# Routed tiles of a mixture of experts: the spreads on SyncE six tiles ahead, and an expert's three weight loads one per tile

## The reference

```python
y = clip(einsum('blc,oc->blo', x * styles, weight) * dcoefs + bias, -256, 256)
shared = silu(xf @ sh_gate_w) * (xf @ sh_up_w) @ sh_down_w        # xf: y as (8192, 512)
topk_idx, w = route(xf)                                            # 8 experts of 64
sorted_x = xf[tok]                                                 # rows sorted by expert
h = silu(ragged_dot(sorted_x, gate_w, sizes)) * ragged_dot(sorted_x, up_w, sizes)
o = ragged_dot(h, down_w, sizes) * w
out = x + shared + zeros.at[tok].add(o)
```

## Time and profile before

| | |
|---|---|
| time, median of 3 runs | 3974.17 us (3964.74 to 3979.28) |
| the profiled execution | 3965.72 us, span 3964.0 us |
| PE, PEld busy | 3733.3 us (94%), 3040.4 us (77%) |
| DVE, ACT, POOL busy | 2235.7 us (56%), 1495.3 us (38%), 1946.4 us (49%) |
| granted TensorE clock, mean | 0.977 of full speed |
| DMA | 550.56 MB, mean 139 GB/s |

### The profile page before, as it was taken

One profiled execution on the slowest core, in us unless ns is written; L12 is line 12 of the kernel. 1 busy time (PEld: TensorE's weight loads), 2 busy tenths in 40 slices (PEclk: granted clock), 3 DMA queues, 4 the chain that ended last, 5 costly groups with the idle time before them and its releaser, 6 DMA issues.

```text
span 3964.0 us, 91393 instructions
## 1 busy us (share of the span) xinstructions
PE 3733.3 (94%) x17024; PEld 3040.4 (77%) x17025; DVE 2235.7 (56%) x4612; ACT 1495.3 (38%) x3339; POOL 1946.4 (49%) x1601
## 2 busy tenths in 40 slices
PE   7999999999999959999999999999999999999987
PEld 5877877878787848878878878787878778777775
DVE  4655555555555645555555555555555555566554
ACT  3222222222222214444444444444444444444443
POOL 1453333333333425655556556555656555555554
PEclk9999999999999979999999999999999999999998
DMA  5121112112111228888889888988888898899887
GB/s 181 51 57 44 44 54 54 44 44 65 44 44 54 44 70 181 182 196 177 177 191 184 182 189 182 200 176 188 178 190 185 187 201 175 194 204 204 198 185 158
DMA packets 589051, 550.56 MB, mean 139 GB/s; under 512 B 133625, under 2 KB 443265, under 8 KB 588929
## 3 DMA queue, kind: packets, MB, share of 16 engines
q0 software_dynamic: 136112, 281.38, 36.5%
q10 hardware_dynamic: 291584, 140.58, 13.9%
q1 hardware_dynamic: 161234, 127.04, 11.7%
HBM read 229.07 MB, written 179.19 MB: 103 GB/s over the span
## 4 chain that ended last, share of the span: by engine, by line
PE 46%; DMA 7%; issue 4%; ACTq 3%; DVE 2%; SPq 1%; DVEq 1%; ACT 1%; POOLq 0%; POOL 0%
PE bank L1231 30%; PE bank L1249 14%; DMA x_split<-x_rows 4%; PE bank L1240 2%; ACTq L1341 2%; DMA raw_d<-in_L_ffn_down_w_dram 1%; DMA out_dram<-o_rows,to_row 1%; DVE w_dn_l L30 1%; DMA lists<-slot_list 1%; DMA x_rows<-y_rows,from_row 1%; DVE x_cols L1407 0%; ACTq L1074 0%; SPq L1074 0%; ACT x_h L1289 0%; DVE w_gu_l L30 0%
## 5 line engine op out<-in xcount | busy, mean ns | idle before, releaser
L1193 POOL DMA_INDIRECT out_dram<-o_rows,to_row x532 | 879.5, 1653 | 278.2 <-issue 230.0
L1177 POOL DMA_INDIRECT x_rows<-y_rows,from_row x539 | 543.9, 1009 | 840.6 <-DMA x_split<-x_rows 605.5
L428 POOL DMA_INDIRECT slot_list<-ent,pos x512 | 503.9, 984 | 862.7 <-PE bank L454 385.4
L1231 PE MATMUL bank<-w_gu_h,x_h 128*128 x2128 | 844.3, 397 | 86.1 <-DVE x_l L30 42.7
L1231 PE MATMUL bank<-w_gu_h,x_l 128*128 x2128 | 840.3, 395 | 0.0
L1231 PE MATMUL bank<-w_gu_l,x_h 128*128 x2128 | 839.7, 395 | 0.0
L1407 DVE STREAM_TRANSPOSE x_cols<-x_split 128x512 f32<-128x512 f32 x535 | 580.1, 1084 | 293.9 <-DMA x_split<-x_rows 293.2
L1414 DVE TENSOR_TENSOR e_hf<-bank,e_sg 128x256 f32<-128x256 f32 x532 | 225.2, 423 | 684.4 <-ACT e_sg L1295 366.2
L1231 PEld LDWEIGHTS bank<-w_gu_h,x_h 128*128 128x128 f32 x2128 | 406.4, 191 | 186.4 <-issue 99.1
L1249 PE MATMUL bank<-w_dn_h,e_h_h 128*128 x1064 | 468.1, 440 | 33.7 <-DVE e_h_l L30 20.5
L1231 PEld LDWEIGHTS bank<-w_gu_l,x_h 128*128 128x128 f32 x2128 | 406.9, 191 | 86.7
(11 more groups left out here) (242 smaller groups left out, 5946.7 us busy)
## 6 DMA issues: line engine op xcount, KB each, us to landing
x_split<-x_rows ACTq DMA_DIRECT2D x1072, 128.0 KB
xin<-in_x_dram SPq DMA_DIRECT2D x16, 1024.0 KB
y_rows<-yrow SPq DMA_DIRECT2D x64, 256.0 KB
stage_d<-in_x_dram SPq DMA_DIRECT2D x16, 1024.0 KB
out_dram<-stage_d SPq DMA_DIRECT2D x16, 1024.0 KB
raw_gu<-in_L_ffn_gate_w_dram SPq DMA_DIRECT2D x29, 512.0 KB
raw_gu<-in_L_ffn_up_w_dram SPq DMA_DIRECT2D x29, 512.0 KB
raw_d<-in_L_ffn_down_w_dram SPq DMA_DIRECT2D x29, 512.0 KB
```

Source lines behind the costliest of these rows:

```text
L428: nc.gpsimd.indirect_dma_start(slots, bass.IndirectOffsetOnAxis(ap=pos[v][:, t, k:k + 1], axis=0), ent[v][:, t, k, :], None).then_inc(scat ...
L1177: nc.gpsimd.indirect_dma_start(xg[u // 2][:, u % 2, :], None, y_rows, bass.IndirectOffsetOnAxis(ap=from_row[u][:].bitcast(U32), axis=0)).t ...
L1193: nc.gpsimd.indirect_dma_start(out, bass.IndirectOffsetOnAxis(ap=to_row[u][:].bitcast(U32), axis=0), og[u][:], None, compute_op=ALU.add).t ...
L1231: last = nc.tensor.matmul(b_gu[u % 2][:], xp[a][:, u % 2, k, :], wgu[b][:, bass.ds(place, 1), k, :].rearrange("p a n -> p (a n)"), start=( ...
```

## The change

The spreads go from ACT's queue to SP's. SP's step j now loads the list of tile j+12, issues for even j the spread of tiles j+6 and j+7, then, in an If of its own each, the down matrix if tile j+4 is the first of its expert, the up matrix if tile j+5 is, and the gate matrix if tile j+6 is. The gather runs eight tiles ahead of POOL's step instead of seven, and rows_from nine instead of eight. The waits are the same as before in each part: the spread waits for both gathers and until tile j+3 is turned.

```diff
-            AHEAD = UN
+            LIST_AHEAD, SPREAD_AHEAD, LOAD_AHEAD = 12, 6, 6
...
+                def spread(j, v, g):
+
+                    for u in (2 * v, 2 * v + 1):
+                        sp.wait_ge(x_ld[u], 16 * (g + 1))
+                        sp.nop(nofuse=True)
+                    if not isinstance(j, int) or j >= UN:
+                        sp.wait_ge(dve_turned, j - 2)
+                        sp.nop(nofuse=True)
+                    for a in range(QD):
+                        sp.dma_start(x_split[v][a * SQ:(a + 1) * SQ, :, :, :].rearrange("c i u e -> c (i u) e"),
+                                     xg[v][:, :, a * P:(a + 1) * P]).then_inc(x_moved[v], 16)
+
-                def weights(j, is_first):
+                def weights(j, is_first, part):
 
                     with sp.If(is_first > 0):
                         order = field(sp, j, 1, E)
                         e = field(sp, j, 2, E - 1)
                         half = order & (RAW - 1)
-                        sp.wait_ge(split, 3 * order + 1)
-                        sp.nop(nofuse=True)
+                        if part == 0:
+                            sp.wait_ge(split, 3 * order + 1)
+                            sp.nop(nofuse=True)
                         if not isinstance(j, int) or j > 0:
...
+                            if part == 0:
+                                sp.wait_ge(raw_gu_ld, 32 * order)
+                                sp.nop(nofuse=True)
+                            if part == 2:
+                                sp.wait_ge(raw_d_ld, 16 * order)
+                                sp.nop(nofuse=True)
+                        if part < 2:
+                            sp.dma_start(raw[0][:, bass.ds(half, 1), :, part * H:(part + 1) * H].rearrange("p a k n -> p (a k) n"),
+                                         (gate_w, up_w)[part][bass.ds(e, 1)].rearrange("e (k p) h -> p (e k) h", p=P)
+                                         ).then_inc(raw_gu_ld, 16)
+                        else:
+                            sp.dma_start(raw[1][:, bass.ds(half, 1), :, :].rearrange("p a k n -> p (a k) n"),
+                                         down_w[bass.ds(e, 1)].rearrange("e (k p) h -> p (e k) h", p=P)).then_inc(raw_d_ld, 16)
...
-                def step(g, u, is_first):
-                    n = g * UN + u
-                    load_list(n, u, g)
-                    weights(n - AHEAD, is_first)
+                def step(g, u, turn):
+                    j = g * UN + u
+                    load_list(j + LIST_AHEAD, (u + LIST_AHEAD) % UN, g + (u + LIST_AHEAD) // UN)
+                    if u % 2 == 0:
+                        spread(j + SPREAD_AHEAD, (u + SPREAD_AHEAD) % UN // 2, g + (u + SPREAD_AHEAD) // UN)
+                    for part in (2, 1, 0):
+                        n = j + LOAD_AHEAD - part
+                        if not isinstance(j, int) or n >= LOAD_AHEAD:
+                            weights(n, turn.first(u + LOAD_AHEAD - UN - part), part)
...
-                    gather(g + 1 + (u + 3) // UN, (u + 3) % UN)
+                    gather(g + 2, u)
...
-                    if u % 2 == 0:
-                        spread(j + UN, u // 2, g + 1)
...
-                    rows_from(j + 2 * UN, u, g + 2)
+                    rows_from(j + 2 * UN + 1, (u + 1) % UN, g + 2 + (u + 1) // UN)
```

More of the change, by code:

```diff
@@ L1127, in weights @@
                         half = order & (RAW - 1)
-                        sp.wait_ge(split, 3 * order + 1)
-                        sp.nop(nofuse=True)
+                        if part == 0:
+                            sp.wait_ge(split, 3 * order + 1)
+                            sp.nop(nofuse=True)
                         if not isinstance(j, int) or j > 0:
-                            sp.wait_ge(raw_gu_ld, 32 * order)
-                            sp.nop(nofuse=True)
-                            sp.wait_ge(raw_d_ld, 16 * order)
-                            sp.nop(nofuse=True)
@@ L1136, in weights @@
-                        for n, w in enumerate((gate_w, up_w)):
-                            sp.dma_start(raw[0][:, bass.ds(half, 1), :, n * H:(n + 1) * H].rearrange("p a k n -> p (a k) n"),
-                                         w[bass.ds(e, 1)].rearrange("e (k p) h -> p (e k) h", p=P)).then_inc(raw_gu_ld, 16)
-                        sp.dma_start(raw[1][:, bass.ds(half, 1), :, :].rearrange("p a k n -> p (a k) n"),
-                                     down_w[bass.ds(e, 1)].rearrange("e (k p) h -> p (e k) h", p=P)).then_inc(raw_d_ld, 16)
@@ L1149, in _ @@
                     if n == 1:
-                        weights(0, field(sp, 0, 3, 1))
+                        for part in range(3):
+                            weights(0, field(sp, 0, 3, 1), part)
+                spread(0, 0, 0)
                 for n in range(UN, 2 * UN):
                     load_list(n, n - UN, 1)
-                for n in range(1, UN):
-                    weights(n, field(sp, n, 3, 1))
-                for n in range(2 * UN, LISTS):
-                    load_list(n, n % UN, n // UN)
-                    weights(n - AHEAD, field(sp, n - AHEAD, 3, 1))
+                    if n == UN + 1:
+                        spread(2, 1, 0)
+                for n in range(1, LOAD_AHEAD):
+                    for part in range(3):
+                        weights(n, field(sp, n, 3, 1), part)
+                for n in range(2 * UN, LIST_AHEAD):
+                    load_list(n, n % UN, n // UN)
+                spread(UN, 0, 1)
+                sp.wait_ge(words, 1)
+                for g in range(2):
+                    turn = Turn(sp, g + 1)
+                    for u in range(UN):
+                        step(g, u, turn)
                 last_turn = field(sp, 0, 5, NTURN - 1)
-                sp.wait_ge(words, 1)
-                with sp.Fori(LISTS // UN, NTURN + 2) as g:
-                    with sp.If(last_turn >= g - 2):
-                        turn = Turn(sp, g - 1)
+                with sp.Fori(2, NTURN) as g:
+                    with sp.If(last_turn >= g):
+                        turn = Turn(sp, g + 1)
                         for u in range(UN):
-                            step(g, u, turn.first(u))
+                            step(g, u, turn)
                 for u in range(UN):
-                    sp.wait_ge(list_ld[u], 16 * last_turn + 48)
+                    sp.wait_ge(list_ld[u], 16 * last_turn + 16 * (1 + LIST_AHEAD // UN))
+                    sp.nop(nofuse=True)
+                for v in range(UN // 2):
+                    sp.wait_ge(x_moved[v], 16 * QD * last_turn + 16 * QD * (3 - v))
                     sp.nop(nofuse=True)
@@ L1202, in _ @@
                 pool.wait_ge(tab_ld, 16)
-                for n in range(UN + 3):
+                for n in range(2 * UN):
                     gather(n // UN, n % UN)
@@ L1330, in end_weights @@
                     weights_high(order, order & (RAW - 1), order & (RING - 1), 2)
-                def spread(j, v, g):
-                    for u in (2 * v, 2 * v + 1):
-                        act.wait_ge(x_ld[u], 16 * (g + 1))
-                        act.nop(nofuse=True)
-                    if not isinstance(j, int) or j >= UN:
-                        act.wait_ge(dve_turned, j - 2)
-                        act.nop(nofuse=True)
-                    for a in range(QD):
-                        act.dma_start(x_split[v][a * SQ:(a + 1) * SQ, :, :, :].rearrange("c i u e -> c (i u) e"),
-                                     xg[v][:, :, a * P:(a + 1) * P]).then_inc(x_moved[v], 16)
                 def step(g, u, turn):
@@ L1356, in step @@
                         end_weights(turn.order(u + 2))
-                    if u % 2 == 0:
-                        spread(j + UN, u // 2, g + 1)
-                spread(0, 0, 0)
-                spread(2, 1, 0)
                 act.wait_ge(words, 1)
@@ L1477, in _ @@
                 turn_x(2, 2, 0)
+                rows_from(2 * UN, 0, 2)
                 turn = Turn(dve, 0)
```

3 lines of the change are left out of this document (2 added, 1 removed).

## The result

| | before | after |
|---|---|---|
| time, median | 3976.73 us (3964.74 to 3986.67, 4 runs) | 4458.65 us (4454.87 to 4464.37, 4 runs) |
| ratio | | 1.1215, 95% interval 1.118 to 1.1249 |
| profiled execution, span | 3965.72 us, 3964.0 us | 4459.48 us, 4457.8 us |
| granted clock, mean | 0.977 | 0.947 |

The change makes the kernel 482 us slower, where 195 us were forecast, with 4440 us as the upper end of the range. All of it lies in the stage of the routed tiles, which is 493 us longer. The first fence is the page's busy times, which answer to the earlier trace rows, and its summary of the chain that ended last; the second the gate/up matmuls (count, ns min/median/max, first and last start), to set beside the earlier trace rows.

A forecast was written before the change was run, and what follows sets the result against it. TensorE bounds the routed-tile stage now (2461 us, some 150 of it stalls); SyncE would become the bound, 531 x 4.5 + 266 = 2656 us, +195. So 3965.7 + 195 = 4160 us, range 3905 to 4440.

The forecast's parts named there:

- part 1: Spread leaves ScalarE: frees 1.47 us a tile there, buys nothing in quiet stretches, helps next to a weight load.
- Part 2: Spread six tiles ahead: some 11.7 us less 2.6 of issue nearly cover a 10.3 us landing; list waits are covered.
- Part 3, the price of an issue: Two spread issues a tile on SyncE: 0.86 us at SyncE's own price, 1.35 at ScalarE's, kept for the range.
- Part 3, the step: SyncE's step with spread issues, two more Ifs, waits and nops: 4.4 to 4.65 us a tile, taken as 4.5.
- the stretch of 1.39: SyncE's quiet step of 2.0 us measured 2.77 a tile, so its work was taken to run 1.3 to 1.39 slower.
- The loads: Weight loads on SyncE: 7.8 to 11.2 us for an expert's three parts; 9.5 x 28 = 266 us taken.
- The sum: SyncE needs 531 x 4.5 + 266 = 2656 us for a 2461 us stage: +195 us, 4160 us.
- the SP case: SyncE becomes the bound of the routed-tile stage: 4160 us, own range 4060 to 4525, chance 0.54.
- A: Rival: SyncE keeps up at 3.6 us a tile, the late spread at loads is covered: 3910 us, chance 0.30.
- B: Rival: SyncE at TensorE's pace, or spreads land late behind loads in its queue (over 12 us): 3966 us, chance 0.16.
- C: Rival: the spread can't run six ahead, as it waits for tile j+3; partly true, in the sums, no chance given.
- The signs that I had named: SyncE's waits shrink from 29 us to nearly none, spread issues back to back, 4.4 us a tile, VectorE/GpSimd awaiting late issues.

The follow-up runs named there:

- e13: The changed kernel run again unedited, on a chip where SyncE's instructions paused: 4442.23 us, 1.1198 of the kernel before.
- e14: The changed kernel with lists 32 deep instead of 16, on a chip with pauses: 4179.68 us, 1.0537 of the kernel before.
- e8: The changed kernel with GpSimd's scatter put ahead of its gather, on a chip without pauses: 4044.87 us, 1.0216 of the kernel before.
- e15: The changed kernel with GpSimd's scatter ahead of its gather, on a chip with pauses: 4220.79 us, 1.0633 of the kernel before.
- e17: The changed kernel run a third time unedited, on a chip without pauses: 4331.81 us, 1.0949 of the kernel before.
- e3: The changed kernel with an expert's three loads in one block behind one If, spreads still on SyncE: 4348.24 us, 1.0973 of the kernel before.
- e10: The kernel before with only GpSimd's scatter put ahead of its gather: 3992.62 us, 1.0089 of the kernel before.
- e11: The changed kernel with an expert's loads in one block and GpSimd's scatter ahead of its gather: 3901.05 us, 0.9851 of the kernel before.
- e12: The changed kernel with lists loaded by ScalarE, loads in one block and GpSimd's scatter ahead of its gather: 3868.09 us, 0.9777 of the kernel before.
- e7: The changed kernel with lists loaded by ScalarE and an expert's loads in one block: 3948.36 us, 0.9962 of the kernel before.
- e1: The changed kernel with lists 32 deep instead of 16, in an earlier comparison, with pauses: 4180.22 us, 1.0530 of the kernel before.

## Why the prediction was wrong, step by step

Where the 482 us went, from runs on one chip (e13, e14): 4442.2 - 3967.7 = 475 us, of which 4442.2 - 4179.7 = 262 us are the ring and 212 us SyncE's run time. What the pauses have in the latter is shown for the other break of the ring: e8 and e15, the same kernel, are +83 us without pauses and +253 with them, 170 us for the pauses. The counts bear out most of the 170: SyncE's work is 0.20 us a tile more in e15 (106 us) and its waits 38 us more. Lists 32 deep were never run without pauses; if 83 us were left there too, 129 of the 212 would be pauses, an estimate. Without pauses (e17, e8) the parts are 292 us of ring and 83 of run time.

**What bounds the kernel, and part 1.** Nothing in the runs speaks against them. That the move off ScalarE buys nothing in the quiet stretch was not tried by itself.

**Part 2, the step that failed.** "Lists are read 12 ahead of SP's step instead of 16 ...; both are covered by three tiles of run-ahead as long as SP isn't late." I took SyncE's wait for the scatters, 785 us, as time to spare. It is a place in a queue: whatever is put behind it on SyncE hangs on a scatter. The term that I put at nothing is the wait for a scatter ahead of each spread, and it is 262 us of the 475 (e13, e14). I costed the wait for the list and for the gather each by itself and never followed them round: list behind scatter, spread behind list, gather behind spread, scatter behind gather. The trace before would have given the lap: a scatter's landing (5.2 us by the median, not among my rows), two of SyncE's steps at my own 4.4 to 4.65 us a tile, a spread's landing of 4.59, and 2 us of GpSimd (not among my rows either): about 21 us against the 17.4 of four tiles. It is 21.3. My own clause "as long as SP isn't late" was broken by my own forecast that SyncE would be late in every turn.

**Part 3, the price of an issue.** I took 0.40 us, that of SyncE's other issues; it is 0.637, ScalarE's 0.645. The price that I kept for the range was right and the value taken wrong.

**Part 3, the step.** All the same SyncE's work a tile came out as forecast. A turn of four tiles without loads takes 17.9 us of work in the changed kernel (the median), 4.48 us a tile; I took 4.5. That is luck, for two errors cancel. Issues and gaps cost 1.33 us where I had 0.86. The two Ifs cost 0.59 by e3 (15.6 us a turn), 0.30 each, which is what I had. By the same count SyncE worked 2.68 us a tile in the kernel before, so 2.68 + 1.33 + 0.59 and my 0.10 to 0.15 for waits and nops would be 4.7. But the 2.68 hold pauses: 278 of some 0.67 us in the stage before are 0.36 us a tile. The changed kernel has 129, 0.19 us a tile less, and 4.7 - 0.19 is the 4.5. I had taken the stretch of 1.39 to grow with the work; where there are no pauses, SyncE works 2.15 us a tile with the spreads on ScalarE (e10), the same additions give 4.2, and e17 has 4.22.

**The loads.** 2.0 to 2.3 us of SyncE for each part, some 6.4 us an expert, where I took 9.5: 180 us, not 266.

**The sum.** 531 x 4.48 + 180 = 2560 us of work. e14, with the ring open, has a stage of 2684 us of which SyncE waits 124, the same 2560. The sum had 2656; the times are +212 us and +195. So "SP becomes the bound" was right in kind, and near in size to what is left when the ring is open (by luck in part, since 129 of those 212 us are pauses by the estimate above). What it left out was the 262 us of the ring. The 4459 us lie inside the 4060 to 4525 that I gave the SP case, but not for its reason: its upper end came from dearer issues and loads.

**The rivals.** A (3910 us, SyncE keeps up) was wrong for this change. e11, where SyncE has the time and no ring, gives 59 us, near the 56 that A had worked out from the late spreads at the loads; no run shows that it is these, and e12 gives more. B rested in part on the order of SyncE's queue. In the changed kernel, whose loads are spread out, a spread issued after them (the last at 1838.60 us) wasn't late, by the chain from 1844 to 1852 us:

```profile
1845.72 4.69 DMA x_split<-x_rows
```

The kernels with one block of loads put it to the test. In e7 a spread is issued right behind three loads, with them still under way; the slowest of this run (SyncE's timeline, then the chain):

```profile
2285.11 0.38 SPq L1141 DMA_DIRECT2D raw_d<-in_L_ffn_down_w_dram  x1
2285.92 3.81 SPq L1121 DMA_DIRECT2D x_split<-x_rows  x4
```

```profile
2289.04 11.42 DMA x_split<-x_rows
```

Of such spreads, whose fourth issue comes within 7 us of all three loads, e7 has 22, which land after 7.7 us by the median (5.3 to 11.4), and e12 22 after 8.2 us (up to 10.7). In the kernel before, 15 of them on ScalarE's queue took 9.7 us (4.7 to 11.3). So sharing the queue with the loads cost nothing that shows, and B's landings of over 12 us came in neither. The Trainium skill, "DMA: Bandwidth & Descriptors", section "Queues, rings and completion order", would let the spread stand behind the loads of its queue. All 44 did land after the last load of their block, but so did the 15 on the other queue, so these traces don't tell the rule from its absence. The Trainium skill, same page, section "Issuing engines are not separate DMA queues", calls the sequencer time usually small; here it is 2.7 us for a pair of tiles, and with the Ifs and loads beside it the bound once the ring is open. C (it can't run six ahead) I had priced by the wait for the turned tile; SyncE hardly ever waits there (1.0 us in all up to 4100 us). It was the wait for the scatter that held it back.

**The signs that I had named.** SyncE's waits in 80 us fell from 29.1 to 5.6, the issues of the spread stand one after another, and VectorE and GpSimd wait for a late issue: all as said, and all true of the ring as well. None told the two apart. What did was the sum over the stage: an engine that is the only bound doesn't wait 280 us for scatters that stand behind its own spreads.

## What to carry to other kernels

An engine's idle time at a wait is only free for work that may hang on that wait: before a step is moved behind one, follow the waits round, write the lap with its number of tiles, and compare it with that many tile times. A lap can be broken in any of its places, and some are cheap: a deeper buffer, or an engine's two steps swapped (which cost 0.9% where there was no ring, e10). When issues are moved to a sequencer, take the price of the same transfer from wherever it is issued now, and count every If that runs in each step, taken or not.

## What the runs showed of the hardware

- The time of an issue went with the transfer, not with the engine: the spread's took 0.645 us on ScalarE and 0.632 to 0.639 on SyncE, beside 0.35 for a list and 0.40 for a load of 512 KB on the same SyncE. So a transfer's size doesn't tell its price: each of the spread's moves 128 KB.
- In the runs on some chips SyncE's register instructions and branches, of 37 to 45 ns by the median, now and then took 0.7 us, 50 to 314 times in a stage; in those on others never. ScalarE's and VectorE's had a few too (23 and 3 in the first trace of the kernel before). The kernel before hardly minds (medians of 3963 to 3969 us beside kernels with pauses, 3956 to 3962 beside those without); the same program whose SyncE is full took 4221 us with and 4045 without. Such a comparison over two chips can mislead: e1 looked 135 us slower than e8, and on one chip it was 41 us faster (e14, e15). What makes the pauses is open. Of those of the changed kernel 88% end while an indirect DMA of GpSimd is at work, which fills 48% of the time, and no run was made to settle it.
- A spread (four transfers of 128 KB each, timed from the fourth issue) took 4.8 to 5.3 us to land by the median away from the loads, and 7.7 to 9.7 us when issued within 7 us of three loads of 512 KB, on the loads' own queue (e7, e12) or on another (before).
